# Unread products in seven pauses of TensorE, in a two-layer decoder kernel

## The reference

```python
x = x + _L0_attn_ref(_layernorm(x), W_q, W_kv, W_o)        # Fourier attention with a cumulative sum
x = x + _L0_xattn_ref(_layernorm(x), k, bias, ctx, ctx, 8) # long convolution, gated by a context
x = x + _L0_ffn_ref(_layernorm(x), W1, b1, W2, b2, W3, b3, Wg, bg)
x = x + _L1_attn_ref(_layernorm(x), Wqa, Wqb, Wkva, Wkvb, Wo)
x = x + _L1_xattn_ref(_layernorm(x), ctx, wq, bq, wkv, bkv, wp, bp)
x = x + _L1_ffn_ref(_layernorm(x), w_gate, w_up, w_down)

# _L0_ffn_ref: 8 experts of three layers, two for each row
gate_weights = softmax(einsum('bsd,dn->bsn', x, Wg) + bg);  topv, topi = top_k(gate_weights, 2)
h = gelu(x @ W1[n] + b1[n]);  h = gelu(h @ W2[n] + b2[n]);  eo = h @ W3[n] + b3[n]
out = sum over the row's two experts of topv * eo

# _L1_attn_ref: 16 heads; q from a latent of 192, k and v from a latent of 64, rotary part of 64, causal softmax
# _L1_xattn_ref: x and two weights rounded to int8 steps, row by row; plain attention over ctx in 16 heads
# _L1_ffn_ref: weights rounded to -1, 0, 1, x to int8 steps; silu(gate) * up, rounded again, times w_down
```

## Time and profile before

| | us |
|---|---|
| median of 3 executions | 723.18 (721.86 to 723.79) |
| the profiled execution, in all | 724.21 |
| its span, first to last instruction | 722.4 |
| PE busy in it | 558.2 (77%) |
| DVE, ACT, POOL busy | 430.5, 300.2, 253.3 |
| mean granted clock of PE | 0.883 |

### The profile page before, as it was taken

How to read it: one execution, slowest core, us unless ns; L and a number is a source line. 1 busy time by engine, 2 the same in 40 slices (tenths; PEclk the granted TensorE clock), 3 DMA queues, 4 the chain that set the end, 5 groups by cost and what they waited for, 6 DMA issues and landing times.

```text
span 722.4 us, 12069 instructions
## 1 busy us (share of the span) xinstructions
PE 558.2 (77%) x4141; PEld 394.7 (55%) x4143; DVE 430.5 (60%) x994; ACT 300.2 (42%) x742; POOL 253.3 (35%) x297
## 2 busy tenths in 40 slices
PE   3949699258369999999979989979888367763665
PEld 2538344156248888887635656656575155643233
DVE  3586899946545555554572544535465647767773
ACT  1421200242534444443423745727573455545553
POOL 3950478854700000000576954908622200010000
PEclk9969999655679999999988999999999789885886
DMA  8592410444751111110220000000000500000000
GB/s 293 171 371 95 145 59 0 150 157 149 243 189 53 46 46 45 46 44 24 81 88 1 1 0 1 1 0 1 1 1 1 175 2 2 2 2 0 8 22 30
DMA packets 32248, 49.62 MB, mean 69 GB/s; under 512 B 3096, under 2 KB 22368, under 8 KB 31808
## 3 DMA queue, kind: packets, MB, share of 16 engines
q1 hardware_dynamic: 29888, 41.65, 17.4%
q0 software_dynamic: 2304, 7.21, 2.8%
HBM read 39.68 MB, written 9.18 MB: 68 GB/s over the span
## 4 chain that ended last, share of the span: by engine, by line
PE 58%; DVE 18%; ACT 12%; POOL 4%; issue 4%; DMA 3%; SPq 0%; ACTq 0%; DVEq 0%; POOLq 0%
PE bank L1565 14%; PE bank L1580 4%; PE bank L1735 4%; PE bank L1675 3%; POOL sorted_rows L499 3%; PE bank L1697 3%; PE bank L1671 2%; PE bank L1724 2%; PE bank L1443 2%; PE bank L1708 2%; ACT sm L722 2%; ACT pT L824 2%; DVE xn L930 2%; PE bank L1980 2%; PE bank L1472 1%
## 5 line engine op out<-in xcount | busy, mean ns | idle before, releaser
L667 ACT ACTIVATE hf<-bank,be 128x256 f32<-128x256 f32 (+1 forms) x120 | 44.3, 420 | 67.4 <-PE bank L1565 53.4
L505 POOL DMA_INDIRECT yg<-expert_rows,pos x16 | 15.8, 988 | 156.0 <-DMA expert_rows<-yb 151.5
L1565 PE MATMUL bank<-h,wsp 128*128 128x256 f16 (+1 forms) x720 | 67.6, 249 | 1.7 <-DVE h L1123 1.6
L1565 PEld LDWEIGHTS bank<-h,wsp 128*128 x720 | 57.2, 97 | 11.1 <-issue 4.8
L1121 DVE CAST h<-hf 128x512 f16<-128x512 f32 (+1 forms) x60 | 21.8, 364 | 56.6 <-ACT hf L667 55.2
L487 POOL TENSOR_TENSOR kvp<-xnT,cxT 128x512 f32<-128x512 f32 x32 | 35.7, 1139 | 42.8 <-issue 33.3
L577 ACT CAST wsp<-wraw 128x2048 f16<-128x2048 f32 x12 | 22.7, 1900 | 66.6 <-DMA wraw<-in_L_ffn_W 66.6
L722 ACT ACTIVATE sm<-sm,nm 128x128 f32<-128x128 f32 x128 | 49.9, 395 | 0.6 <-DVE nm L1236 0.6
L465 POOL TENSOR_TENSOR wsp<-wraw,wsp 128x512 f16<-128x512 f32 x40 | 45.8, 1178 | 9.1 <-ACT wsp L577 8.8
L1233 DVE SCALAR_TENSOR_TENSOR sm<-bank,const 128x512 f32<-128x512 f32 x32 | 22.1, 691 | 38.9 <-PE bank L1697 38.9
L524 POOL TENSOR_TENSOR sm<-sm,rinv 128x512 f32<-128x512 f32 x32 | 33.1, 1040 | 24.9 <-DVE rinv L1227 24.9
(11 more groups left out here) (299 smaller groups left out, 1337.3 us busy)
## 6 DMA issues: line engine op xcount, KB each, us to landing
wraw<-in_L_ffn_W SPq DMA_DIRECT2D x16, 512.0 KB, 5.2
wraw<-in_L_ffn_W SPq DMA_DIRECT2D x8, 1024.0 KB, 7.0
cxT<-in_ctxT SPq DMA_DIRECT2D x2, 1024.0 KB, 7.6
tap<-in_taps SPq DMA_DIRECT2D x1, 2048.0 KB, 14.1
xg<-sorted_rows SPq DMA_DIRECT2D x8, 256.0 KB, 2.8
expert_rows<-yb SPq DMA_DIRECT2D x8, 256.0 KB, 2.2
sorted_rows<-early POOLq DMA_DIRECT2D x1, 1536.0 KB, 13.1
sorted_rows<-early POOLq DMA_DIRECT2D x1, 1408.0 KB, 16.3
```

The lines of the kernel that those rows point to most:

```text
L667: last = nc.scalar.activation(hf[:, p, n * k:n * k + n], bank[2 * (layer - 1) + p][:, n * k:n * k + n], ACT.Gelu, bias=be[:, layer - 1, u, ...
L1565: last = nc.tensor.matmul(b[:, n * (f % 2):n * (f % 2) + n], w[a_][:, c, P * f:P * f + P], inp[:, b_, c, :], start=(c == 0 and a_ + b_ == ...
```

## The change

PE gets a helper, `keep_busy(b, count)`. It writes `count` products into bank b: the bf16 identity `identb`, 128 x 128, as the stationary operand, by itself repeated four times, 512 columns, as the moving one. Nothing reads what they write, and the next real product into that bank starts it anew. They stand in seven places: 26 ahead of the router's transposes, 24 behind the router product, 22 ahead of the experts, 10 and 4 around the first transposes of the latent attention, 12 at the first quantisation and 10 at the second. In three of them a wait stands in front, on a step of another engine, so that they do not begin earlier: the fifth weight split of the DVE, the eighth tile of `xn` of stage 5, and the scales of stage 6.

```diff
@@ block.tensor
+            def keep_busy(b, count):
+
+                for _ in range(count):
+                    nc.tensor.matmul(bank[b][:], identb[:], identb[:].unsqueeze(1).to_broadcast([P, 4, P]), start=True, stop=True)
...
             nc.tensor.transpose(bank[4][:, 0:64], b12[:, :], ident[0:64, 0:64]).then_inc(sem("gate_psum"), 1)
+            keep_busy(7, 26)
             transposes(3)
             all_xnT(3)
...
             last.then_inc(sem("gate_psum"), 1)
+            keep_busy(5, 24)
 
             pe.wait_ge(sem("route_ready"), 2)
...
+            pe.wait_ge(sem("w_split_dve"), 5)
+            keep_busy(4, 22)
             turn_rows(0)
             turn_rows(1)
             pe.wait_ge(sem("w_split"), 10)
...
+            keep_busy(0, 10)
             turn_pair(0)
+            keep_busy(0, 4)
             pe.wait_ge(sem("xnT_act"), 7)
             latents(0)
...
+            pe.wait_ge(sem("xn_ready"), 5 * NT)
+            keep_busy(3, 12)
             pe.wait_ge(sem("sdiag_ready"), NT)
...
+            pe.wait_ge(sem("xn_scaled"), 1)
+            keep_busy(0, 10)
             turn_x(6)
```

## The result

The changed kernel takes 717.98 us (median of 4 executions, 717.65 to 718.83) against 723.48 us (median of 4) of the kernel before beside it: ratio 0.9921, 95% interval 0.9895 to 0.9946. The forecast was 717.5. The profiled execution took 717.78 us with a span of 716.0, against 722.4 before, and its mean granted clock rose from 0.883 to 0.919.

What follows compares the result with a forecast made beforehand. PE bounds the kernel, its slow clock after pauses costing time. Terms 0 + 1.6 + 1.8 + 1.9 + 1.4 = 6.7 us off 724.21 gave 717.5; 5.8 off the median gave 717.4. Forecast 717.5, range 711.0 to 721.5.

Steps and rivals of the forecast that it cites:

- Four microseconds from the first dummy: All pauses: the clock rises 4 us after the first dummy, taken between 3.5 and 4.3.
- The router pair, 0: Around the router product: 26 dummies gain 1.0 us, 24 behind it lose 1.1; together 0.
- The first rival: Router: the clock holds through the product, 5.5 us more gained, 712.0 us; chance 0.16.
- the bound of 3.9 lost: Both router pauses together: at worst 3.9 us lost, against at best 5.5 gained.
- rival 3: All dummies: identity products do not raise the clock, each costs 0.43 us; 9.3 us slower, 732.5 us; chance 0.08.
- rival 2: Behind the router: dummies run cold for long, 3.9 us late, first gain lost; about 721.1 us; chance 0.14.
- The experts, 1.6: Ahead of the experts: 22 dummies warm transposes and first products, net 1.6 us gained, 0.6 taken off for the hole.
- The prediction's sign: Experts: their first product, L1565, would run at clock 1.00 from its start.
- The latent attention, 1.8 here and 0.9 in the median: Latent attention: 1.8 us back from a 3.6 us cold stretch; half that against the median, as the fall may not recur.
- First quantisation, 1.9: First quantisation: 12 dummies end before the scales, no delay; 1.9 us gained, bounds 0.3 and 2.2.
- Second quantisation, 1.4: Second quantisation: 10 dummies end 0.9 us late, warm work saves 2.3; 1.4 us gained, bounds 0.3 and 2.2.
- The falls in the loops only shift.: Last two stages: pauses in the steps stay as they are, and their clock falls and rises only shift.

Runs made afterwards that it cites:

- corner products: The changed kernel with all dummies on a 32 x 32 corner of the identity, 512 columns as before: 729.84 us, ratio 1.0078 to the kernel before.
- router_only: The kernel before with only the 26 and 24 dummies at the router: 723.77 us, ratio 1.0008.
- The five alone: The kernel before with one place's dummies each: router pair 1.0008, experts 0.9999, latent attention 1.0027, first quantisation 0.9967, second 0.9980.

## Why the prediction was right, and where it wasn't

**The sum** of 6.7 us met 6.4 in the spans, the forecast of 717.5 met 717.98. Part of that is luck. The experts' 1.6 did not come, and in the pair of traces the router's 1.15, forecast as 0, stood in for it; that 1.15 is the pattern of the clock on the router product, which came in kernels without router dummies as well. The clock as the cause, and the two quantisations (3.3 forecast, 3.8 by the stretches of all traces), were foreseen and not luck.

**What moves the clock.** Shown. The corner products kept PE busy and left it at 0.50 or let it fall to that; the full-width ones were followed by its rise in all five places where it was low, and in the two of the latent attention it was high and stayed so; transposes alone raised it; the router product let it fall at 153.3. Four microseconds from the first dummy was a fair figure: 4.0 at the router (with the first 0.6 still at 1.00), 3.2 at the experts, 3.7 and 4.1 at the quantisations, 5.4 behind the router product.

**The router pair, 0.** Measured 0 by its removal (0.9923 against 0.9921) and alone (1.0008). In the trace the steps went nearly as written: the fall came early in the product (the prediction's place for it), the 24 were 1.9 us late (162.52 against 160.62, forecast 1.6), and L1503 took 0.56 for 1.12. The first rival, the clock holding through the router, is refuted: it did not in the changed kernel, nor in router_only. What the prediction lacked is that 6.96 was the router product's time in only half of the traces without dummies. It took a single execution for the kernel's, and the earlier trace rows, which it quoted for transposes at 79.1, held the hint that 16 of them may do the same at 149.8. Its premise that the weight splits and the scatters move together behind the router does not hold for a router that is earlier: the fifth split stayed within 0.5 us while the scatters came 1.1 to 2.4 us sooner. Two figures do not follow from its own rates: the bound of 3.9 lost is 5.5 by the 0.8 and 4.7 that rival 3 adds up, and rival 2 turns the 3.9 into 3.7 (721.1 for 721.3).

**The experts, 1.6.** The mis-sized term. The prediction named the hole of 1.60 and took off 0.6 for it; measured alone, the whole gain is gone (0.1 left). In the four traces with the 22 and the hole open the clock fell, so that of the 1.7 us on the first products nothing came (4.46 for 4.47); taking off 0.6 priced about a third of a chance where it was close to certain. The lateness, forecast as 0.2, was some 1.2 us in the changed kernel's trace. Of the gains, only the 0.7 of the transposes came (0.60 and 0.41 us for 1.08 and 0.66). Filling the hole brought 2.0, near the 2.2 that the sum held before the 0.6 was taken off. The prediction's sign that the experts' first product would be at 1.00 from its start failed.

**The latent attention, 1.8 here and 0.9 in the median.** The stretch gave 1.45 in the pair of traces, and the lateness was there and covered as written (360.52, where 1.36 us behind the work before it, as in the earlier trace rows, would be 359.7; the second pair's input at 365.33 came from the DVE). That the fall "was a near thing" is borne out: it appears in two of six traces without the edit, which makes about 0.5 us on average, not 0.9. The slowdown of the kernel with this edit alone is unexplained.

**First quantisation, 1.9.** 2.4 in the pair of traces, 2.4 +- 1.6 alone. The dummies were done 0.85 us ahead of the scales, so the delay of nothing held, and the upper bound of 2.2 was a little low, since the transposes behind it were partly cold before as well.

**Second quantisation, 1.4.** 1.6 in the traces, 1.4 +- 1.5 alone. From the scales to the transposes it was 3.3 us before (662.22 to 665.51) and 4.1 now (657.84 to 661.97): 0.8 late where 0.9 had been forecast.

**"The falls in the loops only shift."** True of the changed kernel, where they moved by 0.35 and 0.3 us. As a judgement of what is worth having it was wrong: the pauses that the change left alone, of the loops and one ahead of the fifth query group, were worth 12.0 us (717.17 to 705.14), twice the change itself. No kernel has them without the others, so what they bring alone is not shown.

**What does not add up.** The five alone make 0.0008 - 0.0001 + 0.0027 - 0.0033 - 0.0020 = -0.0019, or 1.4 us, where together they give 5.7. With about 0.0022 of uncertainty on each that is 1.4 +- 3.6 against 5.7 +- 1.8: at the edge of what the measurement allows. The stretches of the traces make it 2.2 + 1.6 for the quantisations, 0.5 for the latent attention and nothing for the experts with the hole open, 4.3 us, which lies within both. Since every edit shifts the work behind it, it may change which later falls occur; no run here shows that by itself, and it stays open.

## What to carry to other kernels

Unread full-width products pay where a pause ends in dense work of TensorE on the chain, if they end before the input comes and leave no hole behind them. Look for every such pause along the chain, the repeated short ones in loops above all, and fill short holes around transposes too (here 1.60 and 0.83 us). Let the dummies begin with something that moves with the input they must not outlast: the experts' 22 hung on a weight split, and when the rows came earlier they were late. Where the work behind the pause is narrow (here 8 columns), or something long waits for its first instruction, leave them out, and judge each one alone over many executions, since one trace shows one of several patterns of the clock.

## What the runs showed of the hardware that was not expected

- A fully busy TensorE that stayed at 1.2 GHz: 8.00 of 8.00 us at 0.50 with products of 32 x 32 stationary and 512 moving columns, 10.42 us for 24, 0.43 each as the full-width ones when cold.
- The clock fell behind two short holes. In the changed kernel PE stood for 1.60 and 0.83 us between 201.3 and 204.2, with 0.41 us of transposes between, and 0.62 is the clock of the window that follows; with 0.31 and 0.18 it was 1.00.
- The same instructions meet another clock in the next execution: the router product took 6.96 us in the kernel before and 4.62 in the one without router dummies, which differ in nothing up to there. The Trainium skill ("TensorE: Matmul & The Clock Gate", Part 1: The HAM clock gate) says that the number of cold products varies from run to run of one kernel; these traces agree, and the 720.64 to 726.62 us of one kernel's executions go with it.
